# First expert weights of layer 0 brought from DRAM by the sync engine, in place of VectorE's copies from a resident table

## What is computed

```
def _L0_ffn_ref(hidden_states, w_red, wg, W1, b1, W2, b2):
    x = hidden_states.reshape(-1, c)              # 4096 tokens, c = 128
    x_red = x @ w_red
    wg_n = wg / jnp.maximum(jnp.linalg.norm(wg, axis=1, keepdims=True), 0.0001)
    gates = jax.nn.softmax(x_red @ wg_n.T, axis=1)
    scores = jnp.max(gates, axis=1)
    idx = jnp.argmax(gates, axis=1)
    h = jnp.einsum('nc,ech->neh', x, W1) + b1[None]       # W1: 8 x 128 x 256
    h = jnp.take_along_axis(h, idx[:, None, None], axis=1)[:, 0, :]
    h = jax.nn.gelu(h, approximate=False)
    o = jnp.einsum('nh,ehc->nec', h, W2) + b2[None]       # W2: 8 x 256 x 128
    o = jnp.take_along_axis(o, idx[:, None, None], axis=1)[:, 0, :]
    return (o * scores[:, None]).reshape(b, t, c)
```

## Time and profile before

| | us |
|---|---|
| three runs | 805.23, 815.23, 819.42 |
| median of them | 815.23 |
| the profiled execution | 815.39 |
| its span, first to last instruction | 813.7 |
| from the first gather of layer 0's experts to the first gather back | 95.5 to 160.4 |

### The profile page before, as it was taken

The page is one execution under the profiler, slowest core; times in us unless marked ns, Lnnn a source line. Parts: engine busy times, 40 slices in busy tenths (PEclk is TensorE's granted clock), DMA queues, the critical chain, the costliest instruction groups (busy, mean ns, idle before and its releaser), DMA issues.

```text
span 813.7 us, 34138 instructions
## 1 busy us (share of the span) xinstructions
PE 709.0 (87%) x14873; PEld 650.1 (80%) x14874; DVE 640.1 (79%) x1048; ACT 476.6 (59%) x757; POOL 579.5 (71%) x431
## 2 busy tenths in 40 slices
PE   4568778767899999999999999999999998776997
PEld 3357577767788899998899898888999888676897
DVE  6994745379678989999899998999899998866215
ACT  5735234328746756786676677667667764548510
POOL 4811277267789889989889988888788788732750
PEclk8685599999899999999999999999999999985999
DMA  8401324310520000000000000000000000061128
GB/s 336 178 27 53 118 75 96 73 37 9 153 71 13 8 6 6 8 10 6 6 6 8 19 3 3 18 3 3 4 16 4 3 17 17 3 231 56 50 61 293
DMA packets 33583, 42.89 MB, mean 53 GB/s; under 512 B 4000, under 2 KB 25648, under 8 KB 32928
## 3 DMA queue, kind: packets, MB, share of 16 engines
q1 hardware_dynamic: 29856, 33.99, 12.2%
q0 software_dynamic: 3296, 6.76, 3.6%
q10 hardware_dynamic: 288, 0.01, 0.0%
HBM read 26.65 MB, written 14.09 MB: 50 GB/s over the span
## 4 chain that ended last, share of the span: by engine, by line
PE 68%; DVE 12%; issue 10%; POOL 4%; DMA 2%; ACT 2%; DVEq 1%; POOLq 0%; SPq 0%; ACTq 0%
PE psum L1900 18%; PE psum L1955 7%; PE psum L1933 6%; PE psum L2000 6%; PE psum L1991 4%; PE psum L1948 4%; PE psum L1962 4%; PE psum L1970 3%; PE psum L1838 3%; PE psum L1941 2%; PE psum L2258 1%; PE psum L1764 1%; PE psum L1848 1%; DVE small L1430 1%; POOL y_rows L713 1%
## 5 line engine op out<-in xcount | busy, mean ns | idle before, releaser
L1900 PE MATMUL psum<-hT,w_qkv 128*128 128x128 f32 x1408 | 175.7, 282 | 5.8 <-ACT hT L914 2.7
L1900 PEld LDWEIGHTS psum<-hT,w_qkv 128*128 128x128 f32 x1408 | 166.0, 196 | 9.4 <-ACT hT L914 2.8
L617 POOL TENSOR_TENSOR arena<-arena,small 128x1024 f32<-128x1024 f32 x56 | 106.1, 1916 | 40.3 <-DVE small L1449 40.2
L596 POOL TENSOR_TENSOR arena<-arena 128x1024 f32<-128x1024 f32 x56 | 106.8, 1907 | 14.1 <-ACT arena L957 13.1
L582 POOL TENSOR_TENSOR arena<-arena 128x1024 f32<-128x1024 f32 x56 | 106.7, 1905 | 0.1
L1442 DVE TENSOR_REDUCE small<-arena 128x16 f32<-128x1024 f32 x60 | 73.0, 1218 | 12.7 <-ACT arena L946 10.5
L621 POOL TENSOR_TENSOR arena<-arena 128x1024 f32<-128x1024 f32 x28 | 65.9, 2355 | 13.1 <-DVE arena L1469 13.1
L1430 DVE TENSOR_REDUCE small<-psum 128x16 f32<-128x1024 f32 x60 | 72.8, 1215 | 0.2 <-PE psum L2000 0.2
L1436 DVE TENSOR_TENSOR arena<-psum,small 128x1024 f32<-128x1024 f32 x60 | 70.4, 1214 | 0.1
L926 ACT ACTIVATE arena<-psum 128x1024 f32<-128x1024 f32 x28 | 28.7, 1025 | 70.0 <-PE psum L1900 70.0
L558 POOL DMA_INDIRECT arena<-h_rows,route x39 | 39.7, 1018 | 39.2 <-issue 37.7
(11 more groups left out here) (334 smaller groups left out, 1624.0 us busy)
## 6 DMA issues: line engine op xcount, KB each, us to landing
y_rows<-hT SPq DMA_DIRECT2D x8, 512.0 KB, 6.7
arena<-in_L_W_rows SPq DMA_DIRECT2D x2, 2048.0 KB, 10.6
arena<-y_rows SPq DMA_DIRECT2D x8, 512.0 KB, 8.0
o_rows<-arena SPq DMA_DIRECT2D x9, 256.0 KB
x_sb<-in_x_rows SPq DMA_DIRECT2D x4, 512.0 KB, 6.1
arena<-in_L_W_rows SPq DMA_DIRECT2D x2, 1024.0 KB, 9.7
arena<-in_W_in_rows SPq DMA_DIRECT2D x4, 512.0 KB, 14.9
arena<-in_W_out_rows SPq DMA_DIRECT2D x4, 512.0 KB, 9.4
```

What stands on the lines that cost most here:

```text
L596: pool.tensor_tensor(x3, x3, lr[:, tile_of(t) * 32 + k * H:tile_of(t) * 32 + k * H + H].unsqueeze(2).to_broadcast([P, H, D]), ALU.mult).th ...
L617: pool.tensor_tensor(z4, z4, r3.unsqueeze(3).to_broadcast([P, 8, 2, CH]), ALU.mult).then_inc(done, 1)
L1900: mm = pe.matmul(ps[bank][:, p * P:(p + 1) * P], w_qkv[:, j * HD + p * P:j * HD + (p + 1) * P], hT[:, at:at + P], start=True, stop=True)
```

## The change

The table `w1a` and its load are gone. SP now reads each group's packed experts itself (`load_experts`) and, for each of the four tiles, issues a DMA of 128 x 256 values (128 KB) straight from the weights in DRAM into `w1x[u]`, from an address in a register. Groups 0 and 1 are loaded once the packed experts exist. After that, in SP's loop, group g + 2 is loaded once `first_product(g)` has freed its buffer, ahead of `store_group(g)`; both stand in one queue in this order. The semaphore `w1_chosen` is replaced by one for each buffer (`w1_even`, `w1_odd`), and PE waits for all four transfers of a group before its `first_product`.

DVE's copies are gone. In its loop, `rows_out(g)` now comes ahead of `experts_of(g-1)`, and the bias of all four tiles is added in one go.

```diff
-        w1a, w2a, b2a = view(12288, E * F0), view(14336, E * F0), view(18432, E * C)
+        w2a, b2a = view(14336, E * F0), view(18432, E * C)
...
+        w1_in = w1_even, w1_odd
...
-            sp.dma_start(w1a, A["L0_W1_rows"]).then_inc(f0_w, 16)
...
+            def load_experts(g, u):
+                four = sp.value_load(t_exp_i[0:1, ds(g, 1)], min_val=0, max_val=E ** GRP - 1)
+                for t in range(GRP):
+                    at = (((four >> (3 * t)) & (E - 1)) * F0).with_bounds(min_val=0, max_val=(E - 1) * F0)
+                    sp.dma_start(w1x[u][:, t * F0:(t + 1) * F0], A["L0_W1_rows"][:, ds(at, F0)]).then_inc(w1_in[u], 16)
+
+            sp.wait_ge(experts_set, BP + 1)
+            load_experts(0, 0)
+            load_experts(1, 1)
             with sp.Fori(0, LASTG // 2) as i:
                 for u in range(2):
+                    sp.wait_ge(h_mm, (i * 2 + u) * GRP + GRP)
+                    load_experts(i * 2 + u + 2, u)
                     store_group(i * 2 + u, u, 0, GRP)
...
-            def bring_experts(g, u, done):
-                of = experts_of(dve, g)
-                if done is not None:
-                    dve.wait_ge(h_mm, done)
-                for t, e in enumerate(of):
-                    last = dve.tensor_copy(w1x[u][:, t * F0:(t + 1) * F0], w1a[:, ds(e * F0, F0)])
-                last.then_inc(w1_chosen, 1)
...
-            bring_experts(0, 0, None)
-            bring_experts(1, 1, None)
...
                 for g, u, n in ((i * 2 + 1, 1, i), (i * 2 + 2, 0, i)):
+                    rows_out(g, u)
                     of = experts_of(dve, g - 1)
-                    rows_out(g, u)
                     dve.wait_ge(o_stored[1 - u], n * 16 + 16)
-                    add_bias2(g - 1, 1 - u, of, (0, 1))
-                    bring_experts(g + 1, 1 - u, g * GRP)
-                    add_bias2(g - 1, 1 - u, of, (2, 3))
+                    add_bias2(g - 1, 1 - u, of, range(GRP))
+            rows_out(LASTG, 1, USED0 - LASTG * GRP)
             of = experts_of(dve, LASTG - 1)
-            rows_out(LASTG, 1, USED0 - LASTG * GRP)
...
-            def first_product(g, u, m=GRP):
+            def first_product(g, u, n, m=GRP):
+                pe.wait_ge(w1_in[u], n * (16 * GRP) + 16 * GRP)
                 pe.wait_ge(xg_ready, g + 1)
-                pe.wait_ge(w1_chosen, g + 1)
```

More of the change, by code:

```diff
@@ L254, in program @@
         gathered = [sem(f"gathered{u}") for u in range(2)]
-        x_turned, xg_ready, h_mm, hb_ready, hg_ready, w1_chosen, o_mm, o_ready = (
-            sem("ex_" + n) for n in ("x_turned", "xg_ready", "h_mm", "hb_ready", "hg_ready", "w1_chosen", "o_mm", "o_ready"))
+        x_turned, xg_ready, h_mm, w1_even, hg_ready, w1_odd, o_mm, o_ready = (
+            sem("ex_" + n) for n in ("x_turned", "xg_ready", "h_mm", "w1_even", "hg_ready", "w1_odd", "o_mm", "o_ready"))
         o_stored = [sem(f"o_stored{u}") for u in range(2)]
+        w1_in = w1_even, w1_odd
         back_in = [sem(f"back_in{u}") for u in range(2)]
@@ L866, in _ @@
             act.activation(junk, ln_eps, ACT.Gelu)
-            act.wait_ge(f0_w, 64)
+            act.wait_ge(f0_w, 48)
             act.wait_ge(experts_set, BP + 1)
@@ L1279, in _ @@
                 chain.link(dve.tensor_scalar(half_signs[:, k], gates1(j), 0.0, 0.5, ALU.is_ge, ALU.subtract))
-            dve.wait_ge(f0_w, 64)
+            dve.wait_ge(f0_w, 48)
             dve.wait_ge(experts_set, BP + 1)
-            def bring_experts(g, u, done):
-                of = experts_of(dve, g)
-                if done is not None:
-                    dve.wait_ge(h_mm, done)
-                for t, e in enumerate(of):
-                    last = dve.tensor_copy(w1x[u][:, t * F0:(t + 1) * F0], w1a[:, ds(e * F0, F0)])
-                last.then_inc(w1_chosen, 1)
             def add_bias2(g, u, of, tiles):
@@ L1822, in _ @@
             mm.then_inc(ids_mm, 1)
-            pe.wait_ge(f0_w, 64)
+            pe.wait_ge(f0_w, 48)
             pe.wait_ge(experts_set, BP + 1)
@@ L1856, in group_step @@
                 second_product(g - 1, 1 - u, of, (0, 1))
-                first_product(g, u, m)
+                first_product(g, u, n, m)
                 second_product(g - 1, 1 - u, of, (2, 3))
@@ L1861, in _ @@
             turn_x(0, 0)
-            first_product(0, 0)
+            first_product(0, 0, 0)
             with pe.Fori(0, LASTG // 4) as i:
```

## The result

| | before | after |
|---|---|---|
| median of the runs (4 each, one chip) | 810.91 us | 821.37 us |
| lowest and highest | 805.23, 819.42 | 815.63, 826.31 |
| ratio | | 1.0133, 95% interval 1.0081 to 1.0186 |
| profiled execution, its span | 815.39, 813.7 | 826.31, 824.6 |
| first gather of the experts | 95.51 | 97.04 |

The change made the kernel slower. I had forecast 1.2 us less, with a range of 807 to 821 us. On two other chips, measured later against the kernel before, the ratio was 1.0073 (1.0040 to 1.0107) and 1.0085 (1.0052 to 1.0117), while the kernel before against itself gave 1.0038 (1.0007 to 1.0069). So three chips agree on the sign, and the size is about 0.5 to 1.3%, 4 to 11 us; less than 0.4% can't be told from nothing here. In the profiles the stage is 8.4 us longer. That is one execution of each kernel, and the one of the changed kernel was the longest of its four.

A forecast was written before the change was run, and what follows sets the result against it. The prediction took DVE's loop (5.41 us a group) and POOL's gathers (5.22) as nearly tied bounds. It summed -1.6 + 0.4 = -1.2 us against the profiled 815.39 to 814.2, 814.0 as a median, range 807 to 821 us.

The forecast's parts named there:

- What bounds the stage: Experts' stage: the loop through DVE at 5.41 us a group nearly tied with POOL's gathers at 5.22.
- The copies, at nothing: DVE: removing 40 weight copies, 11.8 us of work, gains nothing, since they run where DVE has nothing else to do.
- rival (c): POOL's gathers: the copies had slowed them, so they come faster without; up to 4 us gained, 811; chance 0.04.
- The moved register load, -1.6: DVE's loop: rows_out ahead of the register load makes groups gather-paced and what follows group 9 start 1.6 us earlier.
- The traffic, 0.4: DMA engines: gathers queue behind the added loads, shifting the row of groups once, by 0.4 us.
- The chain of a load, 5.2 us of 6.0: SP's queue: register load, four issues and last landing take 5.2 us, with room for 6.0 before PE needs the weights.
- the 6.3 at which I had put the turn to a loss: SP's load chain: at 6.3 us, a period of 5.36, the change turns into a loss.
- the margin of 0.8: Weight loads: room of 6.0 us less the expected 5.2 leaves 0.8 us, under which the loads cost nothing.
- Beyond it each us costs 0.5 us a group: Weight loads: each us of lateness past the 0.8 us margin costs 0.5 us a group, in 8 groups.
- Rival (a): PE's first product: weights come late; landing 4.7, chain 7.6, period 6.0, time 820.3 us; chance 0.25.
- Rival (b): Gathers: they land 1 us or more later under the loads' traffic and eat the gain; 815 to 816; chance 0.13.
- The Trainium skill's rule: SP's load chain: register load floor about 600 ns, memory latency 2 us at high load; chain 7.3 us, time 819.5.

The follow-up runs named there:

- load_early: The changed kernel with SP issuing each weight load one wait earlier, ahead of the store it stood behind; ratio to the kernel before 1.0014.
- reorder_only: The kernel before with only DVE's rows_out moved ahead of its register load, table and copies kept; ratio 1.0001.
- one_ahead_small: The changed kernel with store and load of a group swapped in SP's queue, and loads of 16 KB in place of 128 KB; ratio 1.0639.
- one_ahead: The changed kernel with store and load of a group swapped in SP's queue, so every group waits for its weights; ratio 1.0736.
- traffic_only: The kernel before, with SP also issuing the changed kernel's loads into memory nobody reads; ratio 1.0022, median 812.18 us.
- early_beside: The kernel load_early, profiled beside the kernel before and the changed kernel on another chip; ratio to the kernel before 1.0013.

## Why the prediction was wrong

- **What bounds the stage: right.** The loop through DVE and the gathers were tied. With DVE's order turned PE waits for gathers, 5.27 us a group.
- **The copies, at nothing: right.** DVE had 11.6 us less to do, to no effect. POOL's gathers kept their 1.00 and 0.30 us, so rival (c) is out.
- **The moved register load, -1.6: right in kind, twice too large.** Measured -0.8 of the stage, and nothing in the time. At group 9 I let the loop's 4.6 us decide; what decided was the last gather, which landed 4.6 us after its issue, not 2.6.
- **The traffic, 0.4: right in kind, 0.8 measured.** The stores' and loads' share of the DMA engines rose from 15.5% to 46.7% between 117 and 147 us, within the 17 to 34 points forecast, and with later gathers the stage of load_early is 0.8 us over that of reorder_only.
- **The chain of a load, 5.2 us of 6.0: this is the step that failed.** Under it I had put the loads at nothing; it measured 6.3 to 7.3 us, at or beyond the 6.3 at which I had put the turn to a loss. Two terms were too small. The landing: "128 KB lies nearest to the first", I wrote, and took the 2.3 us of 16 KB; it measured 2.3 to 3.2, and 16 KB measured 1.6 to 1.9 in one_ahead_small, less than the row I took it from. And SP's part, 2.9: in one_ahead it measured 3.0, but in the changed kernel 3.1 to 5.0, with the turn of SP's loop, 0.5 to 0.7 us at every second group, and single issues of up to 2.24. I had counted such a turn for DVE's loop and forgotten SP's. With it alone the margin of 0.8 at every second group is 0.1 to 0.3.
- **The margin itself: a fault of form.** I compared one number with one number, 0.8 us apart, and gave the late weights 0.25. But my own rows had landings of 2.3 to 4.7 and gathers of 2.6 to 3.5 us. None of the delays was made up: the first products of groups 4, 7 and 9 waited 1.5, 1.9 and 3.1 us, and from group 1 on no distance between two first products fell below 5.2. So the bad groups count, not the usual one. The longest waits stand behind one issue of 2.24 us and one gather of 5.93. The gather, in the chain of waits of the changed kernel:

```profile
127.74 5.93 DMA arena<-h_rows,route
```

- **"Beyond it each us costs 0.5 us a group": too cheap.** It took TensorE's clock as fixed. The waits lowered it, which stretches the products and delays the next load: 5.2 and 6.0 us in place of 4.4 for groups 7 and 9. Of the 1.8 us more that stand behind the start of group 9's first product, most is the clock too: granted 0.70 from 162 to 167 us, where the kernel before had 1.00 in its last products.
- **Rival (a): what happened, its number in part by luck.** It gave a period of 6.0 and 820.3 us, with landings of 4.7 in every group. The period was 6.12 (48.99 over 8) and the stage 8.4 us longer in place of 5.1, but no landing of weights that PE waited for was over 3.2 us: a longer part on SP, a late gather and the clock made up the rest. Rival (b), late gathers, took part in it at group 5, where the transposes waited 2.19 us.
- **The Trainium skill's rule.** From its figures for a register load and for memory latency at high load, the page "DMA: Bandwidth & Descriptors" gave an estimated chain of 7.3 us and an estimated 819.5. The register load measured 0.27 us on SP, under the page's 600 ns, so that term was not there. No run here parts the latency under load from the size of a load, so the page's other term was not tested. By this rule the loads come late: the trace agrees with that, by other terms.

## What to carry to other kernels

Where a prefetch stands in one in-order queue with a store, count its lead from the event that the store waits for, not from the number of groups ahead; here two groups ahead was 6.0 us. Count the turn of the loop on every engine of the chain. If a chain feeds itself, compare its worst case with the room it has, and add what an idle TensorE loses in clock. Taking work off an engine that is not on the chain wins nothing, and paying for it in transfers on a busy DMA can lose.

## What the runs showed of the hardware

One stretch of slow transfers comes back in the same place, at group 5, in the changed kernel (last gather issued at 127.74, turned at 133.71), in traffic_only, in one_ahead and in one_ahead_small (the load of group 5 landed in 6.57 and 4.59 us). In one_ahead it lies between 155 and 164 us, where few transfers are under way (queues, then issues with KB and median us to landing):

```profile
q0 software_dynamic: 96, 0.20, 35.0%
q1 hardware_dynamic: 868, 0.67, 32.5%
issues: line engine op xcount, KB each, median us to landing
arena<-in_L_W_rows SPq DMA_DIRECT2D x4, 128.0 KB, 5.2
arena<-h_rows,route POOLq DMA_INDIRECT x2, 7.0
```

96 packets of gathers took 35.0% of 16 x 9 us, 525 ns each, where the earlier trace rows have 157 (23.8% of 16 x 30 us over 729), at only 96 GB/s. So a landing can come close to three times its usual length while the engines move little. What is slow there was not found. It falls on group 5 in several kernels, and PE waited 2.00 us for the gathers of group 5 in reorder_only too, where no loads were added: that speaks against chance, and against the loads as its only cause. The standstill of DVE of 12 to 19 us on two chips is as open, and so is one execution of early_beside that took 3573.59 us, where its other eleven lie near 847.
